# Decoder kernel: self and cross attention's score steps joined on four row groups, self's z products on the local attentions' banks

## The reference, cut to what matters

```python
x = LN(x + attn(x) @ weight)             # 16 heads of 8, queries = keys = x; values are all of x
x = LN(x + xattn(x, ctx, ctx))           # 16 heads of 8, projections, |i-j| <= 64
x = LN(x + ffn(x))                       # two local-attention layers with an MLP each
# attn:  scores = y y^T / sqrt(8); softmax; o_h = attn_h @ x; concat(o_h) @ weight  (weight: 16 blocks 128x128)
# ffn layer: 8 heads of 64 with normalised and rotated q, k; window of 64; x += o @ wo; x += (a * gelu(g)) @ w2 + b2
```

## Time and profile before

| | |
|---|---|
| median of 3 runs | 1524.27 us (1520.69 to 1526.35) |
| profiled execution | 1524.53 us, its span 1522.7 us |
| busy: TensorE, VectorE, ScalarE, GpSimd | 91%, 66%, 63%, 58% of the span |
| mean granted TensorE clock | 0.962 of 2.4 GHz |
| DMA | 8 GB/s |

### The profile page before, as it was taken

How to read it: one execution, slowest core, us unless ns; L and a number is a source line. 1 busy time by engine, 2 the same in 40 slices (tenths; PEclk the granted TensorE clock), 3 DMA queues, 4 the chain that set the end, 5 groups by cost and what they waited for, 6 DMA issues and landing times. The chain is left out here.

```text
span 1522.7 us, 38533 instructions
## 1 busy us (share of the span) xinstructions
PE 1378.5 (91%) x11993; PEld 939.0 (62%) x12088; DVE 1004.0 (66%) x2900; ACT 952.8 (63%) x2563; POOL 879.9 (58%) x1289
## 2 busy tenths in 40 slices
PE   5889999999999999999999999999999999998764
PEld 3455666666666666666666666666666666666553
DVE  2456677676766767767677677766776767667431
ACT  1246666766766666767666766776667667666542
POOL 1135665567666655666666557666655676666532
PEclk7699999999999999999999999999999999999975
DMA  5000000000000000000000000000000000000000
GB/s 150 8 5 5 5 7 6 5 3 5 2 5 5 5 5 5 3 3 3 5 5 5 5 4 5 2 5 5 5 5 5 3 5 2 5 5 3 3 3 4
DMA packets 22219, 12.47 MB, mean 8 GB/s; under 512 B 5878, under 2 KB 21024, under 8 KB 22176
## 3 DMA queue, kind: packets, MB, share of 16 engines
q1 hardware_dynamic: 21600, 10.90, 2.5%
q10 hardware_dynamic: 576, 1.05, 0.2%
HBM read 9.84 MB, written 2.10 MB: 8 GB/s over the span
## 5 line engine op out<-in xcount | busy, mean ns | idle before, releaser
L807 ACT ACTIVATE local_e<-local_ps,local_bias,local_rn 128x128 f32<-128x128 f32 x512 | 230.6, 521 | 20.4 <-DVE local_bias L981 20.3
L1138 POOL TENSOR_TENSOR local_rn<-local_sc,half_neg 128x8 f32<-128x8 f32 x128 | 212.7, 1662 | 7.5
L1156 POOL TENSOR_TENSOR local_e<-local_e,local_rd 128x512 f32<-128x512 f32 x128 | 133.0, 1039 | 133.5 <-DVE local_rd L985 132.3
L976 DVE TENSOR_REDUCE local_m<-local_ps 128x4 f32<-128x512 f32 x128 | 88.5, 691 | 103.8 <-PE local_ps L664 103.8
L583 PE MATMUL self_ps<-self_z,self_e 128*128 128x129 f32 x1024 | 147.2, 287 | 1.8 <-DVE self_y L910 0.7
L910 DVE SCALAR_TENSOR_TENSOR self_y<-self_ps,self_rd,self_y 128x128 f32<-128x128 f32 x448 | 133.2, 345 | 9.1
L583 PEld LDWEIGHTS self_ps<-self_z,self_e 128*128 128x128 f32 x1024 | 128.6, 195 | 16.1 <-issue 7.3
L1045 POOL TENSOR_SCALAR local_x<-local_out 128x256 f32<-128x256 f32 x32 | 12.9, 404 | 217.0 <-issue 217.0
L807 ACT ACTIVATION_READ_ACCUMULATOR local_e<-local_ps,local_bias,local_rn 128x1 f32 x512 | 137.6, 269 | 0.0
L962 DVE TENSOR_TENSOR local_cosp<-local_ps,cos_t 128x512 f32<-128x512 f32 x128 | 87.0, 679 | 70.5 <-ACT local_sq L790 70.5
L570 PE MATMUL self_ps<-wz,self_kT 128*128 128x512 f32 x256 | 129.4, 631 | 0.5 <-ACT self_kT L750 0.5
(11 more groups left out here) (174 smaller groups left out, 3435.2 us busy)
## 6 DMA issues: line engine op xcount, KB each, us to landing
self_xin<-x SPq DMA_DIRECT2D x32, 64.0 KB, 1.8
cross_cin<-ctx_in SPq DMA_DIRECT2D x32, 64.0 KB, 1.8
out<-local_out SPq DMA_DIRECT2D x32, 64.0 KB, 1.6
wqkv_s<-wqkv SPq DMA_DIRECT2D x2, 768.0 KB
wz<-w_heads ACTq DMA_DIRECT2D x4, 256.0 KB, 5.7
w_r<-w SPq DMA_DIRECT2D x2, 341.0 KB
con<-consts SPq DMA_DIRECT2D x1, 576.0 KB, 6.1
wo_s<-wo SPq DMA_DIRECT2D x2, 256.0 KB
```

Of the source, the lines that this page charges most:

```text
L807: nc.scalar.activation(s.e[:, a, p, :], bank[:, 128 * p:128 * p + 128], ACT.Exp, bias=s.bias[:, a, p:p + 1], scale=s.rq[:, a, p:p + 1], ac ...
L976: nc.vector.tensor_reduce(s.m[:, a, :], bank.rearrange("p (c t) -> p c t", c=LH // 2), AX.X, ALU.max, negate=True)\
L1138: nc.gpsimd.tensor_tensor(s.rn[:, heads], s.sc[:, heads], half_neg[:, 0:LH], ALU.pow).then_inc(done, 8)
L1156: nc.gpsimd.tensor_tensor(s.e[:, a, :, :], s.e[:, a, :, :], s.rd[:, a, :].unsqueeze(2).to_broadcast([128, LH // 2, 128]), ALU.mult)\
```

## The change

1. S and C no longer have a `core16` each. A part J (`joint_scores`) does both in one sequence: first groups 0, 1 of S together with groups 2, 3 of C (`pairs` at index 0), then the other way round. The products of the four groups stand interleaved in program order, in four banks. Each step waits for what both need.
2. z (part Z, `self_values`) goes to the banks of A and B: groups 0, 1 to `LOC[0]`, 2, 3 to `LOC[1]`, between the time when A's (B's) V or rotary products have left the bank and the time when its k or q transposes need it. It waits for `v_ready` or `turned` and `squares`; those transposes wait for ScalarE's copy of z (`z_gone`).
3. A and B are each split in a head (to the transposes of q, k: letters A, B) and a tail (D, E); M and N in a head (shift, moments, transpose: M, N) and a tail (O, P). M's head now runs in pass i for sample i-3, at the end of the pass that did its attention; its tail is at i-4 and B's at i-4, N and P at i-5.
4. All four order strings are new. The number of passes (37) is not changed.

```diff
+LETTERS = ("ADMO", "BENP")
+SKEW = {"S": 1, "C": 2, "A": 3, "D": 3, "M": 3, "O": 4, "B": 4, "E": 4, "N": 5, "P": 5}
+Z_LAG = tuple(STEP * (SKEW[letter] - SKEW["S"]) for letter in "AB")
 ORDER_TENSOR = (
-    "MANAANMNMANMNMCSCBSSBCCSSBCCSABCACSCAASBBCSCBBSCSSCSASBCASSBABAB")
+    "AONOAANOPPSBABPBCZCZBAAJJDDZJJZJBJBJJEEJJDSSDCCSSDCSSDEEMEME")
 ORDER_VECTOR = (
-    "MMNMNNNMAAAAAANMNMCCCBCCBBCCSSBBSSAAANBABBBACSSBBSSACSSBSSCMSCSSSSSCANSB")
+    "NNNNOAAOAPAAPBBABCCCBBBSCCDSDDSSCCDDPEODEPSSSESECCSESSESCSCSSDSMMMSSCMSE")
 ORDER_SCALAR = (
-    "AANMANMCSBCSSABSSBCABACCSBBAASSCCASSBBABBAABBAB")
+    "AOANAPSBBACBZCZBAAZDZDSCBBDCCSSDSSCCEEDDEEDEEEM")
 ORDER_GPSIMD = (
-    "ASMNMNNMCBASASABSAAABBABBBABBANBABCNCSMS")
+    "ANNNSCBAAOABSAAASSBABABBBBBPPDDEEMCCMMSS")
...
-            def head_scores(s, pair):
+            def head_scores(groups):
                 for j in range(GH):
-                    for g in pair:
+                    for s, g in groups:
...
-            def turned_scores(s, pair):
+            def turned_scores(groups):
-                for g in pair:
+                for s, g in groups:
...
+            def joint_scores(v, w):
+                both = [s for s, u in ((SELF, v), (CROSS, w)) if u is not None]
+                pairs = [[(s, g) for s in both for g in s.pairs[n]] for n in range(2)]
...
+                    mask_band(CROSS.even)
+                    mask_band(CROSS.odd)
+                yield
...
+                head_scores(pairs[0])
+                yield
+                if w is not None:
+                    pe.wait_ge(CROSS.max_done, w + 8)
+                    mask_band(CROSS.even)
+                    mask_band(CROSS.odd)
+                yield
+                if v is not None:
+                    pe.wait_ge(SELF.max_done, v + 8)
+                head_scores(pairs[1])
+                yield
...
+                if v is not None:
+                    pe.wait_ge(SELF.neg_ready, v + STEP)
+                turned_scores(pairs[0])
+                yield
+                if w is not None:
+                    pe.wait_ge(CROSS.exp_done, w + 8)
+                    mask_band(CROSS.even)
+                    mask_band(CROSS.odd)
+                yield
+                if v is not None:
+                    pe.wait_ge(SELF.exp_done, v + 8)
+                turned_scores(pairs[1])
                 yield
...
+            def self_values(v):
+                s = SELF
+                for g in range(G):
+                    l = g // 2
+                    u = v - Z_LAG[l]
+                    if g == 0:
+                        pe.wait_ge(s.xT_ready, v + STEP)
...
+                    if behind(v, Z_LAG[l] - STEP):
+                        if g % 2:
+                            pe.wait_ge(LOC[l].turned, u + STEP)
+                            pe.wait_ge(LOC[l].squares, u + STEP)
+                        else:
+                            pe.wait_ge(LOC[l].v_ready, u + STEP)
+                    nc.tensor.matmul(LOC[l].b1 if g % 2 else LOC[l].b0, s.kT[:, :], wz[:, 512 * g:512 * g + 512],
+                                     start=True, stop=True).then_inc(s.z_psum, 4)
                     yield
...
+            def z_gone(l, v, g):
+                w = v + Z_LAG[l]
+                if not isinstance(v, int) or w < STEP * B:
+                    pe.wait_ge(SELF.z_ready, w + 4 * g + 4)
...
                 pe.wait_ge(s.q_roped, v + STEP)
+                z_gone(l, v, 2 * l + 1)
...
                 pe.wait_ge(s.v_ready, v + STEP)
+                z_gone(l, v, 2 * l)
```

More of the change, by code:

```diff
@@ L410, in decoder_kernel, with stages @@
         N_PREP_P = 3
-        def stages(eng, order, prepare_local, self_stage, cross_stage, local_attention, local_mlp):
+        def stages(eng, order, prepare_local, self_stage, cross_stage, attention_head, attention_tail, mlp_head, mlp_tail, joint_scores=None, self_values=None):
             def iteration(i):
                 parts = {}
[L416 to L419, removed]
+                if at(i, SKEW["S"]) is not None:
+                    parts["S"] = self_stage(at(i, SKEW["S"]))
+                    if self_values is not None:
+                        parts["Z"] = self_values(at(i, SKEW["S"]))
+                if at(i, SKEW["C"]) is not None:
+                    parts["C"] = cross_stage(at(i, SKEW["C"]))
+                if joint_scores is not None and (at(i, SKEW["S"]) is not None or at(i, SKEW["C"]) is not None):
+                    parts["J"] = joint_scores(at(i, SKEW["S"]), at(i, SKEW["C"]))
                 for l in range(2):
[L421 to L424, removed]
+                    for letter, part in zip(LETTERS[l], (attention_head, attention_tail, mlp_head, mlp_tail)):
+                        v = at(i, SKEW[letter])
+                        if v is not None:
+                            parts[letter] = part(l, v)
                 weave(order, parts)
@@ new lines, in joint_scores @@
+                yield
+                if v is not None:
+                    pe.wait_ge(SELF.max_done, v + STEP)
+                    nc.tensor.transpose(SELF.even.bitcast(BF16)[:, 0:128], SELF.neg[:, :], ident_b[:, :])\
+                        .then_inc(SELF.neg_psum, STEP)
+                yield
+                if w is not None:
+                    pe.wait_ge(CROSS.max_done, w + STEP)
+                    nc.tensor.transpose(CROSS.even.bitcast(BF16)[:, 0:128], CROSS.neg[:, :], ident_b[:, :])\
+                        .then_inc(CROSS.neg_psum, STEP)
+                    mask_band(CROSS.odd)
@@ new lines, in joint_scores @@
+                yield
+                if w is not None:
+                    pe.wait_ge(CROSS.neg_ready, w + STEP)
+                    mask_band(CROSS.even)
+                yield
+                if v is not None:
+                    pe.wait_ge(SELF.neg_ready, v + STEP)
+                turned_scores(pairs[0])
+                yield
+                if w is not None:
+                    pe.wait_ge(CROSS.exp_done, w + 8)
+                    mask_band(CROSS.even)
+                    mask_band(CROSS.odd)
@@ L560, in self_stage @@
                 yield
[L562 to L574, removed]
                 for n, (h0, hn) in enumerate(SETS):
                     bank = s.b0 if n % 2 else s.b1
+                    if n == 0:
+                        pe.wait_ge(s.z_ready, v + STEP)
                     if n < 2:
@@ L605, in cross_stage @@
                 yield
-                yield from core16(s, v)
                 pe.wait_ge(s.exp_done, v + STEP)
@@ L701, in local_mlp, with mlp_tail @@
                 yield
+            def mlp_tail(l, v):
+                s = LOC[l]
                 pe.wait_ge(s.hT_ready, v + STEP)
@@ L751, in self_stage @@
                 yield
-                for g in range(G):
-                    bank = s.b0 if g % 2 else s.b1
-                    act.wait_ge(s.z_psum, v + 4 * g + 4)
-                    nc.scalar.activation(s.z[:, GH * g:GH * g + GH, 0:128], bank.rearrange("p (j n) -> p j n", j=GH), ACT.Copy)\
-                        .then_inc(s.z_ready, 4)
-                    yield
                 shifts(s, v)
@@ L761, in self_stage, with self_values @@
                     exps(s, v, g)
+                    yield
+            def self_values(v):
+                s = SELF
+                for g in range(G):
+                    bank = LOC[g // 2].b1 if g % 2 else LOC[g // 2].b0
+                    act.wait_ge(s.z_psum, v + 4 * g + 4)
+                    nc.scalar.activation(s.z[:, GH * g:GH * g + GH, 0:128], bank.rearrange("p (j n) -> p j n", j=GH), ACT.Copy)\
+                        .then_inc(s.z_ready, 4)
                     yield
```

82 lines of the change are left out of this document (38 added, 44 removed).

## The result

1516.55 us (median of 20 runs, 1507.20 to 1524.12) against 1525.78 of the kernel before on the same occasions: ratio 0.9942, 95% interval 0.9925 to 0.9959. The change is faster by 0.6%, and the forecast was 1.6%. The runs scatter by 17 us, where those of the kernel before scatter by 6.5, and they go with the mean granted clock: 0.954 in the fastest, 0.941 in the slowest.

A forecast was written before the change was run, and what follows sets the result against it. TensorE was taken to bound the kernel, about an eighth of the pass lost to waits. 26 loop passes at 0.77 us (20.0), plus 4.6 for filling and emptying, tail 0, gave 1499 us, 1.6% faster; range 1450 to 1530.

The forecast's parts named there:

- What bounds it: Loop pass of the kernel before: TensorE bounds it, about 38.8 us of work in 43.76, other 5 us waits.
- the joint steps: Score steps of S and C: four row groups overlap fully, saving 2.9 us of TensorE work a pass.
- rival 3: VectorE's maxima chain lengthens, pass 44.3 us, 1539 us; or four row groups gain nothing, 1559 us; chance 0.13.
- rival 2: Head steps: small bf16 products gain nothing from four groups, 16 take 0.46 us; pass 43.5, 1514 us; chance 0.10.
- The wait chain: New order followed step by step through one pass: waits grow from 5 to 7.1 us, pass becomes 43.0 us.
- Leg b: 9.4 to 22.1 us of the pass, P's residual to C's last maximum: VectorE takes 12.7 us, TensorE waits about 2.1.
- M's transpose waits: End of pass: M's transpose comes 3.1 us after M's shift, held by work ahead on other engines.
- z3's copy behind the table load: ScalarE copies z3 only after loading the exponentials' table, holding B's q transposes till 21.9 us into the pass.
- The rule of the Trainium skill: Tiling speeds TensorE but not PSUM emptying; by it the 2.9 us saved would return as waits for VectorE and ScalarE.
- The sum: Whole kernel: 26 loop passes gain 0.77 us each, 20.0 us, plus 4.6 in filling and emptying, tail 0.
- the 43.8: Distance of self's input transposes: under 42 or over 43.8 us would show the prediction wrong; 43.0 expected.
- Filling and emptying: Eleven passes outside the loop: the joint step saves in six of them at 0.77 us each, 4.6 us.

The follow-up runs named there:

- the one with the shift moved: Changed kernel plus early exponential table, D's second maximum behind C's last, self's second ahead of D's first, M's shift ahead of E's second transpose: 1486.48 us, ratio 0.9756.
- early table and extra products: Changed kernel plus exponential table loaded early on ScalarE and five unread bf16 products per pass in TensorE's waits around the second head step: 1473.35 us, ratio 0.9688.
- the early table: Changed kernel plus a one-column exponential ahead of z2's copy, loading ScalarE's exponential table in idle time: 1475.31 us, ratio 0.9700.
- the extra products: Changed kernel plus eight unread 512-column bf16 products per pass in TensorE's waits around the second head step and B's q transposes: 1485.24 us, ratio 0.9732.

## Why the prediction was wrong

**What bounds it, and the joint steps:** right. In fp32 four row groups overlap as four column groups do in the earlier trace rows, and the part of rival 3 by which nothing is gained is out. The small bf16 products came out in between: 16 of the second head step take 0.33 us (782.47 to 782.80), where 8 took 0.23; forecast were 0.23 to 0.25, and rival 2 had 0.46. The 0.40 that rival 2 works out from the floor of the Trainium skill (TensorE: Matmul & The Clock Gate, "Wait — 56ns, not 53.3ns?") is also more than the 0.33 measured, and the measurement decides.

**The wait chain:** right, to 0.2 us. Forecast 43.0 us a pass, measured 42.79 at full clock. (The working counts 14 wide products a pass; the timeline before has ten, four of z and six of K, Q and V. All steps added up with ten give about 38.6 us, an estimate from the same rows, so the 38.8 and the 5 us of waits stand.) Leg b was 12.7, and is 12.5 (772.95 to 785.4); M's transpose waits 1.03 us, E's A V 0.41, both named. z3's copy behind the table load holds B's q transposes, as said. The rule of the Trainium skill (TensorEngine Tiling (Array Packing), PSUM Bottleneck) that was weighed bore out in part: joining takes 1.96 us a pass off TensorE's steps against the same order with the products apart, and 1.39 of it reach the pass. Of the rest 0.40 is the longer wait of self's first value set for its exponential.

**The sum, at one clock:** this is the step that failed. "26 x 0.77 = 20.0 us in the loop" took for all passes the clock of 1.00 that the earlier trace rows show for one pass of the kernel before, and put what the clock would take at nothing, without a reason. Full passes gain 0.98, 25.5 us over 26. But 22 passes of the profiled execution pay 1.58 to 1.6 for a stretch at 1.2 GHz: 35.3 us lost. Those passes, 44.4 us long, are over the 43.8 that the prediction itself named as a sign of being wrong. In the loop the change is therefore 9.8 us slower (1138.0 to 1147.8 from self's sixth transpose to its last), and no rival had that mechanism; rival 3's pass of 44.3 is as long, but by a longer chain on VectorE, which the trace does not have. The profile before had a hint that I passed over: I counted 5 us of waits a pass and forecast 7.1, of which 2.1 in leg b around the second head step, and the earlier trace rows show what the clock does in thin stretches, 0.69 at the end. The Trainium skill, TensorE: Matmul & The Clock Gate, HAM oscillation — how this bites in real kernels, warns of long gaps without products; here the gaps before a fall are 0.4 to 0.8 us with short bursts between, so that section's rule as worded would not have told it.

**Filling and emptying:** mis-sized, in the other direction. 4.6 us was the term; measured are 13.3 up to self's sixth transpose (212.19 before, 198.88 after) and 7.2 behind its last (172.5 to 165.3), 20.5. What makes it is only in part known. From self's first transpose to its sixth it takes 207.3 us before, 193.1 after, and 205.1 with the products apart; but the granted clock of that stretch goes along, 0.87, 0.93 and 0.88, and other joined kernels take up to 199.9 at 0.89 (the one with the shift moved) and 191.5 at 0.94 (early table and extra products), each in one profiled execution. So some of the 12.0 us between joined and apart is the overlap, and some can be where the low stretches happened to fall. I priced a saved step at its value in the loop; in those passes the clock is low for part of the time (0.77 in 50 to 100 us before, 0.90 after), where four transposes take 0.88 us and not 0.46. That fewer other waits hide a saved step there is argued, not shown.

The three together: 25.5 + 20.5 - 35.3 = 10.7 us, by which the span is shorter. Without falls the profiled execution would have stood near 1478 (1513.75 - 35.3), 21 us under the forecast; with the falls the median stands 18 us above. That the figure came near is luck: errors of opposite sign, 35.3 us too little for the clock against 15.9 too little gain in filling and emptying and 5.5 in the full passes.

## What to carry to other kernels

When a change thins an engine out in a pipelined loop, price the loop twice, at full clock and with one low stretch per pass, and look whether the waits gather at one place. A loop whose pass is as long with a fall as the distance from one fall to the next can, it seems, keep falling in every pass; here 0.43 us more in the pass, as useless work, got it out, and so did filling the waits ahead of the fall, and the early table, which takes the longest of them away and shortens the pass. Cheap first looks are the mean granted clock of all runs, the distances of one instruction over the whole loop (two lengths in one execution tell it at once), and how far behind that instruction each low stretch begins, which names the wait that it follows.

## What was not expected of the hardware

The same program has 42.79 us passes and then 44.37 us passes in one execution, with nothing changed in the data or the order, and 17 us of scatter between executions. In which pass the first fall comes is not explained here. The stretch ahead of the first fall (at 386.03) and the same steps one pass earlier, each seen from self's transpose (370.27 and 327.47):

```profile
382.62:386.03 3.41, 1.81 (x20) 0.79 (x21) 3.41 (x8) 3.15 (x9) 3.41 (x3) 1.00 0.00 0
339.82:343.23 3.41, 1.81 (x20) 0.79 (x21) 3.41 (x8) 3.15 (x9) 3.41 (x3) 1.00 0.00 0
343.23:346.64 3.41, 3.36 (x40) 1.97 (x42) 0.47 (x3) 3.35 (x14) 2.94 (x6) 1.00 0.00 0
```

TensorE was busy 1.81 us in both, the same to 0.01 us on every engine, and only behind the first did the clock fall; behind the other (third row) it stayed at 1.00. So busy time there does not tell the two apart. With the extra products three falls came one behind the other and ended, with early table and extra products two did; only the changed kernel, with its pass of 42.79 and its waits unfilled, kept them to the last pass of the loop.
